# Count matrix of a graph network: the range's first cell added inside VectorE's one-hot compare, in place of shifted edge codes from ScalarE

## The reference

```python
edge_index = jnp.stack([src, dst])
h = jnp.maximum(_layernorm(x, axis=-1), 0.0)
x = x + _L0_gnn_ref(h, L0_gnn_W0, L0_gnn_al0, ..., src, dst)        # two graph attentions of 8 heads
h = jnp.maximum(_layernorm(x, axis=-1), 0.0)
x = x + _L1_gnn_ref(h, edge_weight, src, dst)                       # W[src, dst] = edge_weight, X @ W
h = jnp.maximum(_layernorm(x, axis=-1), 0.0)
x = x + _L2_gnn_ref(h, edge_index, ...)                             # three SAGE convolutions, three dense layers
h = jnp.maximum(_layernorm(x, axis=-1), 0.0)
x = x + _L3_gnn_ref(h, edge_index, L3_gnn_W, L3_gnn_a)              # four attention heads
```

## Time and profile before

| | |
|---|---|
| median of 3 runs | 2128.43 us (2127.01 to 2130.7) |
| the profiled execution's own time | 2128.39 us |
| its span, first to last instruction | 2126.6 us |
| mean granted TensorE clock | 0.938 of full speed |
| busy in the span | PE 1734.2, DVE 1582.6, ACT 1379.3, POOL 305.1 us |
| line 562 (ohc) | 387 instructions, 215.0 us |
| line 564 (ohl) | 387 instructions, 101.4 us |
| line 600 (counting matmuls) | 1161 instructions |

### The profile page before, as it was taken

One profiled execution on the slowest core, in us unless ns is written; L12 is line 12 of the kernel. 1 busy time (PEld: TensorE's weight loads), 2 busy tenths in 40 slices (PEclk: granted clock), 3 DMA queues, 4 the chain that ended last, 5 costly groups with the idle time before them and its releaser, 6 DMA issues. The chain is left out here.

```text
span 2126.6 us, 63582 instructions
## 1 busy us (share of the span) xinstructions
PE 1734.2 (82%) x21987; PEld 1347.7 (63%) x21987; DVE 1582.6 (74%) x3455; ACT 1379.3 (65%) x2350; POOL 305.1 (14%) x451
## 2 busy tenths in 40 slices
PE   4999984598998738899892699998989985488884
PEld 1333333588898628889882466665548984488883
DVE  7998987899999888999998522222332247899996
ACT  0256885999999659999995622221213355799986
POOL 2465511557400030000000000000000000100000
PEclk9999997799999878999996899999999998699997
DMA  2000000010101000011001200000001010000002
GB/s 85 4 1 2 3 2 27 14 40 27 40 31 36 2 26 29 27 40 39 27 27 50 96 1 0 0 0 7 1 13 43 20 61 14 8 21 28 21 22 99
DMA packets 34799, 54.96 MB, mean 26 GB/s; under 512 B 10668, under 2 KB 26240, under 8 KB 34432
## 3 DMA queue, kind: packets, MB, share of 16 engines
q1 hardware_dynamic: 31232, 51.64, 7.2%
q0 software_dynamic: 3328, 0.06, 0.1%
HBM read 43.19 MB, written 8.49 MB: 24 GB/s over the span
## 5 line engine op out<-in xcount | busy, mean ns | idle before, releaser
L1201 PE MATMUL ps<-R,M 128*128 128x132 f16 (+1 forms) x8640 | 826.8, 221 | 190.5 <-DVE M L1120 112.3
L1201 PEld LDWEIGHTS ps<-R,M 128*128 128x128 f16 x8640 | 762.8, 97 | 219.7 <-issue 115.3
L1075 ACT ACTIVATE Rm<-rows,cB 128x1280 bf16<-128x1280 f32 (+3 forms) x816 | 846.9, 1131 | 32.1 <-DVE Mn L1110 18.8
L1209 PE MATMUL ps<-HB,C 128*128 128x66 f16 x6400 | 590.0, 193 | 0.0
L1209 PEld LDWEIGHTS ps<-HB,C 128*128 128x128 f16 x6400 | 571.4, 97 | 0.0
L1120 DVE TENSOR_TENSOR M<-Rm,C 128x1280 f16<-128x1280 bf16 (+3 forms) x816 | 532.5, 678 | 37.1 <-ACT Rm L1075 29.7
L1540 PE MATMUL psA<-R,C 128*128 128x512 f16 (+1 forms) x1200 | 254.1, 351 | 22.1 <-POOL ones L1574 9.5
L600 PE MATMUL acc<-ohc,ohl 128*128 128x420 f16 (+1 forms) x1161 | 246.1, 348 | 26.5 <-DVE ohl L564 23.9
L562 DVE TENSOR_SCALAR ohc<-cells,near 128x1280 f16<-128x1280 f16 x387 | 215.0, 556 | 28.3 <-PE acc L600 24.2
L1123 DVE SCALAR_TENSOR_TENSOR M<-rows,cN,C 128x1280 f16<-128x1280 f32 (+1 forms) x144 | 217.7, 1512 | 0.0
L600 PEld LDWEIGHTS acc<-ohc,ohl 128*128 128x128 f16 x1161 | 89.4, 97 | 175.3 <-DVE ohl L564 120.9
(11 more groups left out here) (294 smaller groups left out, 2318.2 us busy)
## 6 DMA issues: line engine op xcount, KB each, us to landing
rows<-rowd SPq DMA_DIRECT2D x32, 640.0 KB, 3.8
rows<-rowd SPq DMA_DIRECT2D x16, 320.0 KB, 3.4
xd<-R SPq DMA_DIRECT2D x4, 640.0 KB, 2.9
xr<-xd SPq DMA_DIRECT2D x20, 128.0 KB, 2.1
xd<-HB SPq DMA_DIRECT2D x1, 2560.0 KB, 8.1
xr<-xd SPq DMA_DIRECT2D x5, 512.0 KB, 5.4
R<-in_x SPq DMA_DIRECT2D x1, 2432.0 KB
xr<-in_x SPq DMA_DIRECT2D x19, 128.0 KB, 2.0
```

The costliest lines, as they stand in the source:

```text
L1075: a.activation(Rm[:, s % SG, 0:wide(p)], rows[:, p % 2, 0:wide(p)], ACT.Relu, bias=cB[:, ds(h + s * nh, 1)]).then_inc(s_R, 1)
L1201: m = pe.matmul(region(p % 2, r), lhsT, rhs, start=first, stop=True, skip_group_check=True)
L1209: m = pe.matmul(both[:, :, cw:2 * cw], C[:, s * NP + p * W + r * P:][:, 0:P], VP[:, s, :, ds(h * cw, cw)], start=False, stop=True, skip_gr ...
```

## The change

ScalarE's shifted codes and their tile `near` go. base holds +1280 q in place of -1280 q. VectorE's compare for ohc, in the same instruction, first adds base[q] to the cell numbers and then compares with the unshifted code of the edge: `(cells + base[q]) == codeT[k]`, which is true where `cells == codeT[k] - base[q]`. Both base[q] and codeT[k] are read as one scalar per partition.

```diff
-                g.iota(base[:, :], pattern=[[-CELLS, NW]], base=0, channel_multiplier=0,
+                g.iota(base[:, :], pattern=[[CELLS, NW]], base=0, channel_multiplier=0,
...
-            near = ph.sb("near", [P, 2, NG * P], f32)
...
-            s_oh, s_used, s_out, s_D, s_sq, s_late, s_near = (
-                ph.sem(n) for n in ("oh", "used", "out", "D", "sq", "late", "near"))
+            s_oh, s_used, s_out, s_D, s_sq, s_late = (ph.sem(n) for n in ("oh", "used", "out", "D", "sq", "late"))
...
-
-                def close_codes(q):
-                    a.activation(near[:, q % 2, :], codeT[:, :], ACT.Identity, bias=base[:, q:q + 1]).then_inc(s_near, 1)
-
-                for q in range(2):
-                    close_codes(q)
                 a.sem_inc(s_late, 4)
...
-                    if q + 2 < NW:
-                        close_codes(q + 2)
...
-                    v.wait_ge(s_near, q + 1)
                     with v.Fori(0, threes) as i:
                         for u in range(U3):
                             k = chunk(first + i * U3 + u, NG * P - 1)
                             v.wait_ge(s_used, (before + i) * U3 + u + 1)
-                            v.tensor_scalar(ohc[:, u, :], cells[:, :], near[:, q % 2, ds(k, 1)], None,
+                            v.tensor_scalar(ohc[:, u, :], cells[:, :], base[:, q:q + 1], codeT[:, ds(k, 1)], ALU.add,
                                             ALU.is_equal).then_inc(s_oh, 1)
```

## The result

| | before | changed |
|---|---|---|
| median | 2128.43 us (2126.9 to 2130.7, 5 runs) | 2139.43 us (2136.91 to 2142.06, 5 runs) |
| ratio | | 1.0054, 95% interval 1.0043 to 1.0065 |
| span of the profiled execution | 2126.6 us | 2139.5 us |

The account below looks back on a forecast made before the run. VectorE's pace, 0.62 us per chunk, was taken to bound the counting stretch, except once per range, where TensorE's psD matmuls do. +23.2 - 7.2 - 1.0 = +15.0 us on 2128.39 us gave 2143.4 us, range 2132 to 2151.

Parts of the forecast that it names:

- The price: VectorE's ohc compare: reading a second scalar per partition adds 60 ns per chunk, bounds 0 and 70.
- The second operation is free: VectorE's ohc compare: adding before comparing costs nothing, as two rows of 0.24 us each showed.
- Gross: All 387 ohc compares on VectorE, before anything is hidden: 387 x 0.060 = 23.2 us more.
- The start: Start of the counting stretch: VectorE's first ohc no longer waits for ScalarE's shifted codes, -1.0 us.
- ScalarE: ScalarE's 40 activations, 24.6 us, go; they were hidden behind its own waits, so removing them brings nothing inside the loop.
- What is hidden: Once per range, VectorE's wait for TensorE's psD chain absorbs 0.18 us of slower compares: 40 x 0.18 = 7.2 us.
- The counts that I gave as tests: ohc's waits for TensorE would fall to about 17 us instead of 24.2, still some 60 of them.
- B: VectorE's ohc compare: the second scalar is free, 0 ns; only the start's -1.0 us is left, 2127.4 us; chance 0.09.
- C: VectorE's ohc compare falls to half its element rate, 333 ns more each: +103.7 us, 2232 us; chance 0.07.
- D: ScalarE was the hidden bound at every range's end, so its 24.6 us come off: -9.6 us, 2118.8 us; chance 0.03.
- the case that sets all 24.2 us against the price: Upper bound of absorption: all 24.2 us of VectorE's waits for TensorE take up the slower compares' time.

## Why the prediction was right, and which term was off

**The price.** Right: 60 ns forecast from one row, line 390, and measured as 61 ns in the pace and 58 and 59 ns in the duration, on two instructions of different width. The second operation is free, as lines 304 and 305 had it. Gross 23.5 us, forecast 23.2.

**The start.** Right: 1.02 us, forecast 1.0.

**ScalarE.** Right: nothing, with or without its 40 activations.

**What is hidden.** The failed step is "From the ohl of a range's third chunk (303.60) TensorE's chain fixes when the next ohc but three may start (306.14)", with its 40 x 0.18 = 7.2 us. Measured 12.3. It took the earlier trace rows's "0.42 <-PE acc L600" at its word. At that place, the start of a range of six, the gap is VectorE's own chain of register instructions. By place, the time over the pace fell so from before to changed: 6.4 us at range starts (19.1 to 12.6), 2.8 at the seventh chunk of the 20 longer ranges (9.7 to 6.9), 0.9 one chunk behind it, and 2.2 at all others. The first is the register chain's (two chunks of 0.061 us at each of 39 starts would be 4.8), the second psD's, and for the last two I have no experiment. The counts that I gave as tests said so at once: waits for TensorE of 17 us in some 60 places were forecast, and 7.4 in 21 stand in the profile. That the sum came out within 4 us is partly luck: the mechanism was wrong at the range starts, and its size per range, 0.18 us against 0.31, was not far off. The range starts alone hid 6.4 us, near the 7.2 forecast; what the sum left out is a second stall in the 20 longer ranges (2.8 us) and the 3.1 us without an experiment.

**The rivals.** B (free) fell with 607 ns, C (slower by element) with the same number, D with ScalarE's work put back. The time lies between the forecast and the case that sets all 24.2 us against the price.

## What to carry to other kernels

Of the scalars of a VectorE instruction in a loop, those known when the program is written belong in it as constants: each one read per partition was 60 ns here, as long as the instruction itself is short enough for that to count. Where an idle gap stands between one loop and the next, look at the engine's own sequencer between the two instructions before believing the engine that the profile names, and try it by adding a few semaphore increments there. Register work behind the loop's end costs nothing while compute still runs beside it, so splitting it over two places can be worth as much as the change one set out to judge: 11 us here.

## What the runs showed of the hardware

A second scalar per partition adds 58 and 59 ns to a VectorE instruction at 128 and at 1280 elements (248 to 306, 548 to 607 ns), and 61 ns to the distance of starts. A second operation added nothing at 16 bits (548 ns with one and with two). A load of a register from the table kept VectorE's sequencer for 0.32 us in the median of forty, and semaphore increments in a row stood 0.093 us apart on it. More work on VectorE's compares shortened the gaps at the range starts twice, by 6.4 and by 7.7 us in all; with what the other places hid, 12.3 us each time, 11 and then 9 us of two gross steps of some 23.5 us reached the end.
